# A recurrent layer with a channel-mixing layer behind it: the Vector engine's residual additions at the end of the step, their statistics in the next

## The chip, the cores and the metric

The kernel runs on one core of one Trainium2 chip. A time is the device time of one execution of the whole program in microseconds (us). Three executions of the kernel before took 246.79, 247.10 and 247.14 us; their median is 247.1.

The engines are named as the profile names them: PE is TensorE (PEld its weight loads), DVE is VectorE, ACT is ScalarE, POOL is GpSimd, SP is SyncE.

## The reference

The input x is 8 sequences of 512 tokens with 128 channels, in float32. Two layers are applied, each as "x plus the layer norm of the layer's result for the layer norm of x":

```python
x = x + _layernorm(attn(_layernorm(x)))     # gated linear recurrence, 32 heads
x = x + _layernorm(ffn(_layernorm(x)))      # token shift and channel mixing
...
# attn: proj = x @ W_in gives z, x_raw, B, C, dt, lambda, theta
x_raw = silu(x_raw); Bm = rms(Bm) * bias; Cm = rms(Cm) * bias   # B and C then turned by an angle (cumulative sum of dt * theta)
y = y_intra + y_inter                       # within a chunk, and from the state carried between chunks
y = rms(y * silu(z)); return y @ W_out
...
# ffn
xr = mu_r * x + (1 - mu_r) * x_prev; xk = mu_k * x + (1 - mu_k) * x_prev
r = sigmoid(xr @ W_r.T); k = xk @ W_k.T
out = r * (square(relu(k)) @ W_v.T)
```

The first "x plus" is the residual addition that this case is about. Its result is normalized again for the second layer, for which a mean and a variance of every token are needed.

## The kernel before, in words

**Tiles and groups.** The work is cut into 32 tiles of 128 rows: a tile holds a chunk of 64 tokens of two sequences. Four tiles (one chunk position c of all 8 sequences) are a group; there are 8 groups. Everything stays in SBUF: `x_all` holds x and later x after the first layer, `o_all` the first layer's result and later the output.

**Steps.** After a preparation of some 50 us each engine runs its own program of steps, one for a tile, n = 0 to 31, with q = n % 4. All instruction orders are written out by hand; the engines meet only through semaphores. On DVE a step does this, in this order:

- for tile n: `mask` (L1405, the scores by the causal mask, `sg`); for tile n-1: `gated_y` (L1424, `y`) and `state` (L1413, `sp`)
- `ffn(n)`: work of the second layer and of the seam between the layers, one part for each q
- for tile n+1: `weighted_x`, first half (L1398, `x`); for tile n+2: `biased` (L1381, `bc`); for tile n+1 the second half (L1398, `xg`)
- in a step with q = 3: `mix` (L1509, `curT` and `prevT`, the token shift of the group two back), which PE's product with the key weights (L1114) waits for
- for tile n+2: `rotations` (L1386 `rot`, L1391 `turned_bc`).

**The parts of `ffn` on DVE.** With c = n // 4:

- q = 0: `moments(c - 2)`: L1488 aggregates the statistics, L1490 adds epsilon; POOL then takes the power -1/2 (L500, `frs`)
- q = 1: `norm_biases(c - 2)` (L1499, `fnb`) and, from n = 17 on, `last_residual(c - 4)` (L1531, four additions into `o_all`)
- q = 2: `factor_terms(c - 1)` (L1460 to L1464, `tokc`), and from n = 14 on `gated_v` and `stats3` (L1518, L1525)
- q = 3: `residual(c - 1)` (L1471: four instructions, each x plus a factor by o, for one tile of 128x128) and `stats2(c - 1)` (L1477: four statistics of the sums). This holds for n = 7, 11, 15, 19, 23 and 27. Groups 6 and 7 are done at the end, by other calls.

**What the x product hangs on.** `weighted_x` for tile n+1 reads the bank into which PE projects tile n+1 (L876, three products) and on which ACT applies silu (L667). PE may start that projection only when DVE has released the bank with the second half (`xg`) for tile n. So there is a ring DVE, PE, ACT, DVE, gone round once in a step. PE does other work in between: the turn of B and C (L940), the projection of B, C and z (L868), the turn of y (L1062, after DVE's `y`), the mixing (L975, L963, L969), the scores (L954) and the output (L1071).

**POOL** has in each step the lower part of the projected tile (L430), a power (L458), the weights `wx` (L466), the product for `zs` (L473, two tensors in SBUF) and the new state `st` (L481, the same). **ACT** has in a step with q = 3 also the scaled copies for `mix` (L746, `behind`). Its squares (L656) wait for DVE's `bc` and are the first link of POOL's power and `wx` of that step.

Of the kernel before, what the change touches and what calls it, by code (L numbers as in the profile page):

```python
# [31 lines left out]
NC_ = T // L  # L32
NQ = B // 2
# [54 lines left out]
def build(nc, x, w_in, a_log, dt_bias, bc_bias, w_out, w_r, w_k, w_v, mu, consts, out, force_general=False):  # L88
    ctx = ExitStack()
    with ctx:  # L90
# [6 lines left out]
        def at(buf, i):  # L97

            if isinstance(i, int):
                return buf[:, i, :]  # L100
            return buf[:, bass.ds(i, 1), :].rearrange("p a n -> p (a n)")

        def wait_past(eng, semaphore, value):

            if not isinstance(value, int) or value > 0:
                eng.wait_ge(semaphore, value)
# [106 lines left out]
        def within(n):  # L213

            return not isinstance(n, int) or 0 <= n < NT
# [15 lines left out]
        def carries(i):  # L231

            return not isinstance(i, int) or i < NT - NQ
# [69 lines left out]
        def valid(c):  # L303

            return 0 <= c < NC_
# [5 lines left out]
        def lo(u):  # L311
            return UNITS[u][0]

        def hi(u):

            return UNITS[u][1] if u >= 0 else 0
# [21 lines left out]
        def n_of(u):  # L338
            return hi(u) - lo(u)
# [8 lines left out]
        def column2(i):  # L348

            return i // NQ % 2 * 2 * NQ + i % NQ  # L350

        def column3(i):
            return column2(i) + NQ
# [4 lines left out]
        for u2, u3 in ((7, -1), (8, -1), (-1, 5), (-1, 6), (-1, 7), (-1, 8)):  # L358
            first, n = (column2(lo(u2)), n_of(u2)) if u2 >= 0 else (column3(lo(u3)), n_of(u3))
# [8 lines left out]
        def last_use(k):  # L368

            for j in range(k - 1, -1, -1):  # L370
                if rounds[j][0] < rounds[k][1] and rounds[k][0] < rounds[j][1]:
                    return j + 1, hi(rounds[j][2]), hi(rounds[j][3])
            return 0, 0, 0

        def aggregated(k):

            return sum(r[1] - r[0] for r in rounds[:k + 1])
# [849 lines left out]
        def _(dve):  # L1227
# [155 lines left out]
            def rotations(n, q):  # L1383
                dve.wait_ge(S["bc_ready"], n + 1)

                vec.tensor_tensor(rot[:], bc[:].rearrange("p (g a n) -> p g a n", g=G3, a=2).unsqueeze(3)  # L1386
                                  .broadcast_to([128, G3, 2, 2, H]),
                                  at(cs_all, n).rearrange("p (a j n) -> p a j n", a=2, j=2).unsqueeze(1)
                                  .broadcast_to([128, G3, 2, 2, H]), ALU.mult).then_inc(S["rotated"], 1)
                dve.wait_ge(S["rotated"], n + 1)  # L1390
                vec.tensor_tensor(turned_bc[:, q].rearrange("p g (j n) -> p g j n", j=2), rot[:, :, 0], rot[:, :, 1],  # L1391
                                  ALU.add).then_inc(S["bc_turned"], 1)
# [63 lines left out]
            def factor_terms(u):  # L1456
                t = tiles_in(u)
                dve.wait_ge(S["o_sb"], hi(u))
                dve.wait_ge(S["ysq_done"], hi(u))
                vec.scalar_tensor_tensor(out=tokc[:, 1, t], in0=ysq_all[:, t, 0], scalar=EPS_LN, in1=osq_all[:, t, 0],  # L1460
                                         op0=ALU.mult, op1=ALU.add).then_inc(fac_v, 1)
                vec.tensor_tensor(tokc[:, 2, t], csq_all[:, t, 0], eps_all[:, t], ALU.add).then_inc(fac_v, 1)
                dve.wait_ge(fac_v, FAC_STEPS * u + 2)
                vec.scalar_tensor_tensor(out=tokc[:, 6, t], in0=tokc[:, 2, t], scalar=EPS_LN * EPS_RMS * SCALE2_INV,  # L1464
                                         in1=tokc[:, 1, t], op0=ALU.mult, op1=ALU.add).then_inc(fac_v, 1)

            def residual(u):

                dve.wait_ge(fac_p, u + 1)
                for i in range(lo(u), hi(u)):  # L1470
                    vec.scalar_tensor_tensor(out=x_all[:, i], in0=o_all[:, i], scalar=tokc[:, 7, i:i + 1],  # L1471
                                             in1=x_all[:, i], op0=ALU.mult, op1=ALU.add).then_inc(C["x1"], 1)

            def stats2(u):
                for i in range(lo(u), hi(u)):
                    dve.wait_ge(C["x1"], i + 1)
                    vec.bn_stats(fst[:, column2(i)], x_all[:, i]).then_inc(C["stats"], 1)  # L1477

            def moments(k):

                used, n2, n3 = last_use(k)
                wait_past(dve, C["norm_bias"], used)
                wait_past(dve, C["pow"], used)
                wait_past(dve, C["stats"], hi(rounds[k][2]))
                wait_past(dve, C["stats3"], hi(rounds[k][3]))
                t = slice(rounds[k][0], rounds[k][1])
                for j in range(t.start, t.stop):
                    vec.bn_aggr(fag[:, j], fst[:, j]).then_inc(C["agg"], 1)  # L1488
                dve.wait_ge(C["agg"], aggregated(k))
                vec.tensor_scalar(fmo[:, t], fag[:, t, 1], EPS_LN, None, ALU.add).then_inc(C["mom"], 1)  # L1490

            def norm_biases(k):

                used, n2, n3 = last_use(k)
                dve.wait_ge(C["pow"], k + 1)
                wait_past(dve, C["normed"], n2)
                wait_past(dve, C["outv"], n3)
                t = slice(rounds[k][0], rounds[k][1])
                vec.scalar_tensor_tensor(out=fnb[:, t], in0=fag[:, t, 0], scalar=-1.0, in1=frs[:, t], op0=ALU.mult,  # L1499
                                         op1=ALU.mult).then_inc(C["norm_bias"], 1)  # L1500
# [12 lines left out]
            def gated_v(u):  # L1513
                dve.wait_ge(C["th"], u + 1)
                dve.wait_ge(C["v_ps"], u + 1)
                wait_past(dve, C["res"], hi(ahead(u)))
                for k, i in enumerate(range(lo(u), hi(u))):
                    vec.scalar_tensor_tensor(out=ff[:, slot(i)], in0=th[:, slot(i)], scalar=1.0,  # L1518
                                             in1=ffn_bank("v", u)[:, k * D:k * D + D],
                                             op0=ALU.add, op1=ALU.mult).then_inc(C["f"], 1)  # L1520
# [6 lines left out]
            def last_residual(u):  # L1527
                dve.wait_ge(C["pow"], round3(u) + 1)
                dve.wait_ge(C["x1"], hi(u))
                for i in range(lo(u), hi(u)):  # L1530
                    vec.scalar_tensor_tensor(out=o_all[:, i], in0=ff[:, slot(i)], scalar=frs[:, column3(i):column3(i) + 1],  # L1531
                                             in1=x_all[:, i], op0=ALU.mult, op1=ALU.add).then_inc(C["res"], 1)

            def ffn(n):
                c, q = divmod(n, NQ)
                if q == 0 and valid(c - 2):
                    moments(c - 2)
                if q == 1 and valid(c - 2):
                    norm_biases(c - 2)
                if q == 1 and valid(c - 4):  # L1540
                    last_residual(c - 4)
                if q == 2 and valid(c - 1):
                    factor_terms(c - 1)
                if q == 2 and valid(c - 3):
                    gated_v(c - 3)
                    stats3(c - 3)
                if q == 3 and 0 <= c - 1 < NC_ - 2:
                    residual(c - 1)
                    stats2(c - 1)

            def last_ffn(general):
                stats2(6)
# [37 lines left out]
            def step(n, q, general):  # L1590
                if within(n) and not general:
                    mask(n)
                if within(n - 1):
                    if general:
                        tokens_general(n - 1, (q - 1) % NQ, (q + 1) % 2)
                    gated_y(n - 1, (q - 1) % NQ, (q + 1) % 2, general)
                    if not general and carries(n - 1):
                        state(n - 1, (q - 1) % NQ)
                if within(n) and general:
                    mask(n)  # L1600
                ffn(n)
                if within(n + 1):
                    weighted_x(n + 1, (q + 1) % 2, 0)
                if within(n + 2) and not (isinstance(n, int) and n == -2):
                    biased(n + 2)
                if within(n + 1):
                    weighted_x(n + 1, (q + 1) % 2, 1)
                if q == NQ - 1 and valid(n // NQ - 2):
                    mix(n // NQ - 2)
                if within(n + 2):  # L1610
                    rotations(n + 2, (q + 2) % NQ)

            biased(0)

# [57 lines left out]
```

## Time and profile before

| | |
|---|---|
| median of three runs | 247.1 us |
| the profiled execution: its own time | 247.12 us |
| its span, from the first to the last instruction | 245.3 us |
| around the span | 247.12 - 245.3 = 1.82 us |
| mean granted clock of TensorE | 0.960 |
| DVE busy / PE busy | 210.7 us (86%) / 208.8 us (85%) |
| ACT busy / POOL busy | 181.3 us (74%) / 142.4 us (58%) |

The page divides the span into 40 slices of 6.1 us. From the slice at 116 us to the one that ends at 202 us DVE's digits are all nines, which means 90% busy or more; PE's are nines and a few sevens. The chain that ended last holds only three pieces at the end of the program, so it says nothing of the middle; the steps have to be read from the timelines. In a timeline a row is a run of equal instructions of one engine. The duration of an instruction runs until its result is out; the next one on DVE usually starts 0.07 to 0.1 us before that. A bracket gives the idle time of the engine ahead of the row and what ended it.

### The profile page before, as it was taken

How to read it: one execution, taken by the hardware profiler on the slowest of the kernel's cores; microseconds unless marked ns; L12 is line 12 of the kernel's file. 1: busy time of each engine (PE TensorE's matmuls, PEld its weight loads, DVE VectorE, ACT ScalarE, POOL GpSimd, SP SyncE). 2: the span in 40 equal slices, each digit the busy share in tenths (PEclk: the TensorE clock that was granted, in tenths of full speed). 3: DMA queues.
4: the chain of work that ended last, by engine and by line, in shares of the span. 5: the costliest groups of instructions: out<-in, count | busy, mean ns of one | idle time of the engine just before them, and what ended most of it. 6: DMA issues, size and time to landing. Idle time of an engine off the chain costs nothing. (4 is left out here: it accounts for less than half of the span.)

```text
span 245.3 us, 6409 instructions
## 1 busy us (share of the span) xinstructions
PE 208.8 (85%) x1902; PEld 156.1 (64%) x1902; DVE 210.7 (86%) x658; ACT 181.3 (74%) x697; POOL 142.4 (58%) x241
## 2 busy tenths in 40 slices
PE   0895997589999999979979997999799799949930
PEld 0893443357777776758857875787588577627920
DVE  1799999987879987996999999999999998864880
ACT  2466685639988689778977896899789879747661
POOL 7444225646777696766757765766777576046230
PEclk9999799989999999999999999999999999986995
DMA  5980000000000000000000001001000100100223
GB/s 119 233 283 1 3 0 0 1 0 4 3 1 4 0 3 0 4 1 3 3 3 0 3 4 44 3 0 45 3 3 0 43 5 4 43 0 0 45 52 88
DMA packets 10199, 6.45 MB, mean 26 GB/s; under 512 B 864, under 2 KB 9856, under 8 KB 10160
## 3 DMA queue, kind: packets, MB, share of 16 engines
q1 hardware_dynamic: 10016, 5.77, 9.1%
q8 instruction: 18, 0.29, 0.5%
q0 software_dynamic: 144, 0.21, 0.4%
q14 instruction: 21, 0.17, 0.2%
HBM read 3.88 MB, written 2.10 MB: 24 GB/s over the span
## 5 line engine op out<-in xcount | busy, mean ns | idle before, releaser
L975 PE MATMUL bank<-x,sg 64*64 64x256 f32 x256 | 35.4, 396 | 0.0
L667 ACT ACTIVATE bank<-bank,rsn 128x512 f32<-128x512 f32 x32 | 21.1, 659 | 17.0 <-PE bank L876 17.0
L975 PE MATMUL bank<-xg,sg 64*64 64x256 f32 x256 | 33.0, 376 | 0.0
L963 PE MATMUL pair<-x,turned_bc 64*64 64x256 f32 x224 | 31.1, 397 | 0.0
L1398 DVE TENSOR_TENSOR x<-bank,wx 128x512 f32<-128x512 f32 x32 | 21.8, 682 | 7.3 <-ACT bank L667 7.3
L458 POOL TENSOR_TENSOR rb<-mse,halfn 128x2 f32<-128x2 f32 x32 | 24.8, 773 | 2.5
L500 POOL TENSOR_TENSOR frs<-fmo,halfn 128x8 f32<-128x8 f32 (+2 forms) x13 | 15.1, 1158 | 17.2 <-DVE fmo L1490 17.2
L1071 PE MATMUL bank<-wo_sb,yt 128*128 128x128 f32 x128 | 23.3, 306 | 1.9 <-ACT yt L683 1.9
L430 POOL TENSOR_TENSOR x_lo<-xnT_all,x_hi 128x128 fp32r<-128x128 f32 x32 | 14.8, 463 | 17.0 <-ACT x_hi L582 16.9
L656 ACT ACTIVATE junk<-bank 128x64 f32<-128x64 f32 x64 | 13.9, 228 | 11.2 <-DVE bc L1381 8.7
L975 PEld LDWEIGHTS bank<-xg,sg 64*64 64x64 f32 x256 | 18.0, 134 | 6.3 <-issue 0.2
L473 POOL TENSOR_TENSOR zs<-zs,ec_all 128x256 f32<-128x256 f32 x32 | 22.0, 687 | 0.0
L975 PEld LDWEIGHTS bank<-x,sg 64*64 64x64 f32 x256 | 15.4, 135 | 10.1 <-issue 6.1
L1398 DVE TENSOR_TENSOR xg<-bank,wx 128x512 f32<-128x512 f32 x32 | 21.7, 679 | 0.0
L455 POOL TENSOR_TENSOR mse<-msb,eps_all 128x2 f32<-128x2 f32 x32 | 7.4, 233 | 24.0 <-ACT junk L658 23.8
L481 POOL TENSOR_TENSOR st<-sp,f_all 128x256 f32<-128x256 f32 x28 | 18.1, 646 | 5.4 <-DVE sp L1413 5.4
L876 PE MATMUL bank<-w_hi,x_hi 128*128 128x512 f32 x32 | 17.2, 536 | 3.8 <-DVE w_lo L1282 2.7
L1071 PEld LDWEIGHTS bank<-wo_sb,yt 128*128 128x128 f32 x128 | 17.1, 194 | 4.7 <-ACT yt L683 2.1
L969 PE MATMUL bank<-st,bt 64*64 64x256 f32 x128 | 19.4, 379 | 0.6 <-DVE o_all L1333 0.6
L954 PEld LDWEIGHTS pair<-bt 64*64 64x64 f32 x256 | 16.9, 132 | 4.4
L954 PE MATMUL pair<-bt 64*64 64x64 f32 x256 | 18.0, 217 | 0.0
L1386 DVE TENSOR_TENSOR rot<-bc,cs_all 128x384 f32<-128x384 f32 x32 | 17.6, 550 | 0.0
(200 smaller groups left out, 712.0 us busy)
## 6 DMA issues: line engine op xcount, KB each, us to landing
x_all<-x SPq DMA_DIRECT2D x16, 128.0 KB, 3.7
out<-o_all SPq DMA_DIRECT2D x14, 128.0 KB, 2.5
cm<-consts SPq DMA_DIRECT2D x1, 640.0 KB, 5.6
w_sb<-w_in SPq DMA_DIRECT2D x1, 480.0 KB, 4.6
out<-o_all SPq DMA_DIRECT2D x4, 64.0 KB, 2.1
cm<-consts POOLq DMA_DIRECT2D x1, 128.0 KB, 3.9
wo_sb<-w_out SPq DMA_DIRECT2D x1, 128.0 KB, 4.7
bcb_sb<-bc_bias SPq DMA_DIRECT2D x1, 96.0 KB, 3.7
```

The source lines that it names most:

```text
L458: nc.gpsimd.tensor_tensor(rb[:, par], mse[:], halfn[:, 0:R], ALU.pow).then_inc(S["rb_ready"], 1)
L473: nc.gpsimd.tensor_tensor(zs[:, q].rearrange("p (h e) -> p h e", e=P), zs[:, q].rearrange("p (h e) -> p h e", e=P), at(ec_all, n).unsqueez ...
L481: nc.gpsimd.tensor_tensor(st[:, q].rearrange("p (h e) -> p h e", e=P), sp[:].rearrange("p (h e) -> p h e", e=P), at(f_all, i).unsqueeze(2) ...
L667: nc.scalar.activation(x_ps[:], x_ps[:], ACT.Silu, scale=rsn[:, par:par + 1]).then_inc(S["x_silu"], 1)
L876: mm = nc.tensor.matmul(x_ps[:], a[:, par], b[:, O_X:O_S], start=(k == 0), stop=(k == 2))
L954: mm = nc.tensor.matmul(scores[half(h), r], bt[half(r), par, r, half(h)], bt[half(r), par, 1 - r, half(h)], start=True, stop=True)
L963: mm = nc.tensor.matmul(p_ps[half(1 - h)], turned_bc[half(h), q, 2 * r], rx(x, r)[half(h)], start=(r == 0), stop=(r == R - 1))
L969: mm = nc.tensor.matmul(y_ps[par][half(h)], bt[half(1 - h), par, h, half(h)], state[half(1 - h)], start=True, stop=stop)
L975: mm = nc.tensor.matmul(y_ps[par][half(h)], sg[half(h), a, r], rx(x, r)[half(h)], start=start, stop=stop)
L1071: mm = nc.tensor.matmul(o_ps, yt[:, k], wo_sb[:, k], start=(k == 0), stop=(k == 1))
L1386: vec.tensor_tensor(rot[:], bc[:].rearrange("p (g a n) -> p g a n", g=G3, a=2).unsqueeze(3) .broadcast_to([128, G3, 2, 2, H]), at(cs_all, ...
L1398: vec.tensor_tensor((x1, xg)[a][:, par].rearrange("p (a e) -> p a e", e=P), x_ps[:].rearrange("p (a e) -> p a e", e=P), wx[:, par, a].unsq ...
```

## The change

In the steps with q = 3 the four residual additions leave the front (behind `sp`) and go to the end (behind `turned_bc`). Their four statistics go to the next step, q = 0, directly ahead of the aggregation. Only DVE's order is changed; the orders of PE, ACT, POOL and SP stay, and no instruction is added or removed.

```diff
             def ffn(n):
                 c, q = divmod(n, NQ)
                 if q == 0 and valid(c - 2):
+                    if c - 2 < NC_ - 2:
+                        stats2(c - 2)
                     moments(c - 2)
...
-                if q == 3 and 0 <= c - 1 < NC_ - 2:
-                    residual(c - 1)
-                    stats2(c - 1)
...
             def step(n, q, general):
...
                 if within(n + 2):
                     rotations(n + 2, (q + 2) % NQ)
+                if q == NQ - 1 and 0 <= n // NQ - 1 < NC_ - 2:
+                    residual(n // NQ - 1)
```

The front of a step with q = 3 on DVE, as the order of instructions has it (`sp` is the new state's sum, `x` the first half of the x product, `bc` the biased B and C):

```order
 L1424 TENSOR_TENSOR y<-bank,zs 128x256
 L1413 TENSOR_TENSOR sp<-pair,st 128x256
-L1471 SCALAR_TENSOR_TENSOR x_all<-o_all,tokc,x_all 128x128 x4
-L1477 BN_STATS fst<-x_all 128x6 x4
 L1398 TENSOR_TENSOR x<-bank,wx 128x512
 L1381 TENSOR_TENSOR bc<-bank,bcb_sb 128x192
```

The additions and statistics are gone from between `sp` and the x product.

The end of the same step and the front of the next on DVE (`turned_bc` is the last instruction of the step before; `sg` and `y` open the next step, `fag` is the aggregation):

```order
 L1386 TENSOR_TENSOR rot<-bc,cs_all 128x384
 L1391 TENSOR_TENSOR turned_bc<-rot 128x192
-L1405 TENSOR_TENSOR sg<-pair,cm 128x256
-L1424 TENSOR_TENSOR y<-bank,zs 128x256
-L1413 TENSOR_TENSOR sp<-pair,st 128x256
+L1471 SCALAR_TENSOR_TENSOR x_all<-o_all,tokc,x_all 128x128 x4
+L1405 TENSOR_TENSOR sg<-pair,cm 128x256
+L1424 TENSOR_TENSOR y<-bank,zs 128x256
+L1413 TENSOR_TENSOR sp<-pair,st 128x256
+L1477 BN_STATS fst<-x_all 128x6 x4
```

The additions now stand between `turned_bc` and `sg`, and the statistics between `sp` and the aggregation.

## Rows read from the trace of the kernel before

**Rows 1.** The page's part 1: busy us, share of the span, instructions, by engine.
```profile
PE 208.8 (85%) x1902; PEld 156.1 (64%) x1902; DVE 210.7 (86%) x658; ACT 181.3 (74%) x697; POOL 142.4 (58%) x241
```

**Rows 2.** Windows: busy us (instructions) by engine, clock, DMA share, GB/s; one group.
```profile
122.00:144.30 22.30, 20.89 (x225) 16.41 (x225) 22.09 (x69) 18.05 (x78) 15.57 (x28) 1.00 0.01 2
```

**Rows 3.** Timeline of DVE, step 15: start us, us, engine, line, work, [idle].
```profile
122.60 0.42 DVE L1413 TENSOR_TENSOR sp<-pair,st 128x256 f32<-128x256 f32 x1
122.93 1.89 DVE L1471 SCALAR_TENSOR_TENSOR x_all<-o_all,tokc,x_all 128x128 f32<-128x128 f32 x4
124.75 0.86 DVE L1477 BATCH_NORM_STATS2 fst<-x_all 128x6 f32<-128x128 f32 x4
125.53 0.67 DVE L1398 TENSOR_TENSOR x<-bank,wx 128x512 f32<-128x512 f32 x1
...
126.98 0.74 DVE L1509 SCALAR_TENSOR_TENSOR curT<-bank,mu_sb,behind 128x512 f32<-128x512 f32 x1
127.64 0.74 DVE L1509 SCALAR_TENSOR_TENSOR prevT<-bank,mu_sb,behind 128x512 f32<-128x512 f32 x1
...
128.87 0.44 DVE L1391 TENSOR_TENSOR turned_bc<-rot 128x192 f32<-128x192 f32 x1
...
129.57 0.41 DVE L1424 TENSOR_TENSOR y<-bank,zs 128x256 f32<-128x256 f32 x1
```

**Rows 4.** Timeline of ACT, the same step.
```profile
123.45 0.66 ACT L667 ACTIVATE bank<-bank,rsn 128x512 f32<-128x512 f32 x1 [0.66 <-PE bank L876]
...
124.50 1.27 ACT L746 ACTIVATE behind<-bank,one_less_mu 128x512 f32<-128x512 f32 x2
125.64 0.40 ACT L683 ACTIVATE yt<-bank 128x256 f32<-128x256 f32 x1
126.49 0.22 ACT L656 ACTIVATE junk<-bank 128x64 f32<-128x64 f32 x1 [0.45 <-DVE bc L1381]
```

**Rows 5.** Timeline of PE's matmuls and weight loads, steps 15 and 16.
```profile
128.43 1.12 PE L1114 MATMUL bank<-curT,wk_sb 128*128 128x512 f32 x2 [1.41 <-DVE prevT L1509]
...
130.71 0.34 PEld L1062 LDWEIGHTS bank<-cm,y 128*128 128x128 f32 x2
```

**Rows 6.** Timeline of DVE: x's first product in steps 9, 10, 13, 17, 29; curT.
```profile
92.12 0.69 DVE L1398 TENSOR_TENSOR x<-bank,wx 128x512 f32<-128x512 f32 x1 [0.82 <-ACT bank L667]
...
97.36 0.69 DVE L1398 TENSOR_TENSOR x<-bank,wx 128x512 f32<-128x512 f32 x1 [1.17 <-ACT bank L667]
...
114.06 0.69 DVE L1398 TENSOR_TENSOR x<-bank,wx 128x512 f32<-128x512 f32 x1 [1.79 <-ACT bank L667]
...
136.40 0.68 DVE L1398 TENSOR_TENSOR x<-bank,wx 128x512 f32<-128x512 f32 x1
...
203.31 0.69 DVE L1398 TENSOR_TENSOR x<-bank,wx 128x512 f32<-128x512 f32 x1 [0.92 <-ACT bank L667]
...
213.06 0.75 DVE L1509 SCALAR_TENSOR_TENSOR curT<-bank,mu_sb,behind 128x512 f32<-128x512 f32 x1 [1.22 <-ACT behind L746]
```

**Rows 7.** Timeline of POOL, steps 15 and 16.
```profile
123.01 0.76 POOL L473 TENSOR_TENSOR zs<-zs,ec_all 128x256 f32<-128x256 f32 x1
123.73 0.68 POOL L481 TENSOR_TENSOR st<-sp,f_all 128x256 f32<-128x256 f32 x1
...
128.35 0.75 POOL L466 TENSOR_TENSOR wx<-w_all,rb 128x128 f32<-128x128 f32 x1
129.06 0.74 POOL L473 TENSOR_TENSOR zs<-zs,ec_all 128x256 f32<-128x256 f32 x1
```

**Rows 8.** Line L1471 in step 15, then behind step 30: durations ns min/median/max.
```profile
L1471 DVE SCALAR_TENSOR_TENSOR x_all<-o_all,tokc,x_all x4: 339/533/726, 122.9 to 124.5; 128x128 f32<-128x128 f32 x4
...
L1471 DVE SCALAR_TENSOR_TENSOR x_all<-o_all,tokc,x_all x4: 338/342/343, 210.0 to 210.8; 128x128 f32<-128x128 f32 x4
```

**Rows 9.** Timeline of DVE at the end: the statistics directly ahead of their aggregation.
```profile
214.39 0.86 DVE L1477 BATCH_NORM_STATS2 fst<-x_all 128x6 f32<-128x128 f32 x4
215.45 0.64 DVE L1488 BATCH_NORM_AGGREGATE fag<-fst 128x2 f32<-128x6 f32 x8 [0.20 <-DVE fst L1477]
```

## The prediction

> **What bounds the kernel now.** First the page's busy shares [rows 1]: DVE 86% and PE 85%, so neither idles much, and the shares alone do not tell which of them an idle piece would hurt. The chain that ended last is of no use here. So I went to the windows: a group of four steps with all of the second layer's work takes 22.3 us, and in it DVE is busy for 22.09 and PE for 20.89 [rows 2]; the two groups behind it look alike. From step 15 to step 28 DVE has no gap at all in its timeline. PE has about 1.4 us to spare in a group, and it spends them in one place: ahead of the key's product, which waits for DVE's `prevT` (1.41 us idle) [rows 5]. ACT and POOL are well below. So from step 15 to step 28 each 0.1 us that DVE idles or works longer counts, unless a later idle place swallows it. Such places are the x products of steps 9, 10 and 13 (0.82, 1.17 and 1.79 us idle, waiting for ACT's silu), of step 29 (0.92), and `curT` behind step 31's work (1.22) [rows 6]. In step 17 the x product at 136.40 waits for nothing, because `last_residual` fills that place from there on.
>
> **The change part by part.** I number by step 15, whose rows are shown.
>
> 1. The x product comes too early. The additions and statistics stood in front of it, from 122.93 to 125.53, 2.60 us [rows 3]. They covered the wait for silu, which ended at 123.45 + 0.66 = 124.11 [rows 4]; DVE follows 0.03 later (in step 13 the like is seen), at 124.14. Now DVE gets there at 122.93 and idles 124.14 - 122.93 = 1.21 us.
>
> 2. Then `curT`. It stands 126.98 - 125.53 = 1.45 behind x, which would be 125.59. It needs ACT's `behind`, done at 124.50 + 1.27 = 125.77 [rows 4], say 125.80. Another 0.21. Together DVE is 1.42 us late.
>
> 3. The aggregation now stands right behind the statistics that it waits for. Elsewhere a successor on DVE starts some 0.08 us before the end of the instruction ahead; at the end of the kernel, where this very pair stands together, the statistics end at 214.39 + 0.86 = 215.25 and the aggregation starts at 215.45 after 0.20 idle [rows 9]. So the pair costs 0.20 to 0.28 us; I take 0.25, once a group. From above the bound is that 0.28, from below nothing. For steps 16, 20 and 24: 3 x 0.25 = 0.75.
>
> The Trainium skill says otherwise: in "VectorE: DVE Perf Modes", section "The DRAIN you can't avoid", a semaphore after each operation is told to cost nothing over having it only after the last, since the pipe is emptied anyway. By that the 0.75 would be 0 and the sum 247.25, the first rival. The trace has the 0.20 us gap on exactly this pair, so the row decides.
>
> 4. Whom the additions meet. Four additions take 338 to 343 ns each where POOL is idle, behind step 30, and 339 to 726 in step 15 [rows 8]. Started 0.26 apart they would need 1.05 us; in step 15 they hold the engine for 124.75 - 122.93 = 1.82, so 0.77 are lost. The two long ones end just behind POOL's `zs` (123.01 + 0.76) and `st` (123.73 + 0.68) [rows 7]. I read it so: an addition with two SBUF tensors and a POOL instruction on SBUF tensors take turns. At the new place `wx` and `zs` are due. POOL's `wx` starts 128.35 - 125.53 = 2.82 behind x, `zs` 3.53 behind it to 4.27 [rows 3, 7], and both hang on DVE's `bc` through ACT's squares, so they move along with x. The additions will start 128.87 - 125.53 + 0.28 = 3.62 behind x: into the end of `wx` and the whole of `zs`. In step 15 itself the squares cannot start before ACT's `yt` is over at 126.04 [rows 4], so POOL is later by some 0.8 and both meetings are whole. Bounds for a group: -0.77 (no meeting) to +0.4 (held up by `wx` in full and `zs` in full, and `turned_bc` too). I take +0.1 for each of steps 15, 19 and 23: 0.3. The same instructions in `last_residual` meet POOL before and after; I take no change.
>
> 5. What is gained. The statistics no longer stand ahead of the next step's `sg` and `y`: 125.53 - 124.75 = 0.78, and `turned_bc` no longer collides with `wx` (128.87 to the next at 129.23, 0.36 where 0.28 is usual): 0.86 in all. PE's turn of y starts at 130.71, though `y` was there at 129.57 + 0.41 = 129.98 [rows 3, 5]: PE was 0.73 late because it had waited for `prevT`. With the additions and statistics no longer ahead of it, `prevT` comes 2.60 earlier, less the lateness of DVE, so PE has its key's product behind it in time and takes y as it comes. So this point of PE stands at DVE's lateness - 0.86 - 0.73.
>
> **Paid once, not in each group.** Once DVE is 1.42 late to PE, the x product of step 19 finds silu done: PE stands at 1.42 - 0.86 - 0.73 = -0.17, so silu's end is not later than before, 1.21 behind DVE's old arrival, and DVE arrives 1.42 or more later than that. The cover that the additions gave is now given by DVE's own lag. The same holds for steps 23 and 27. The lag of steps 7 and 11 never gets that far: 1.42 + 0.25 = 1.67 is less than 0.82 + 1.17 and less than 1.79, the idle times behind them [rows 6]. I count 0.0 for both.
>
> **The sum.** At step 28's turn of y on PE: 1.42 + 0.75 + 0.30 - 0.86 - 0.73 = +0.88 us. From there to the end PE leads. DVE is late by 1.42 + 0.25 x 4 + 0.1 x 4 = 2.8; step 29's x product absorbs 0.92 of that, so 1.9 is left, and the wait of 1.22 ahead of `curT`, whose end moves with PE by 0.88 (together 2.1), takes it. The end then hangs on ACT's `behind` as before. So +0.9 on the profiled execution's 247.12 (span 245.3 and 1.82 around it), which is the median of 247.1 within 0.02: **248.0 us**.
>
> **The rivals.**
>
> - *Nothing that can be measured.* The aggregation waits for nothing more (0 for 0.75), or the additions meet POOL a little less: 247.12 + 0.88 - 0.75 = 247.25. For it: only 0.13 us separates it from a change too small to see, and gains and losses here are of one size. Against it: the gap of 0.20 at the very same pair [rows 9].
> - *Faster.* The additions slip past POOL. One mechanism: `wx` and `zs` are over before `turned_bc`, or both start only behind the additions. Then a group gains 0.77; with four of them up to step 28, 0.88 - 0.30 - 4 x 0.77 = -2.5, that is 244.6. It shows in the median of L1471 near 345 ns instead of 530. It decides from two groups on. For it: the new place has no `st`, which waits for `sp` of the next step. Against it: `zs` at 3.53 to 4.27 behind x, the additions at 3.62.
> - *Much slower: the stall is paid in each group.* If PE is held back by DVE's lateness as much as DVE is late (for instance because the projection waits for `xg` in steps 16 to 18 and silu moves too), 1.21 + 0.21 come again in steps 19, 23 and 27: 3 x 1.42 = 4.3 on top, 252.3. For it: DVE has no spare time in the group. Against it: PE's 1.4 us of spare time [rows 5], which is more than the 0.88.
>
> **How the numbers follow.** A difference of 0.2%, 0.5 us, is about what a measurement of this kernel tells from no change. Forecast (247.5 to 249.0 as its own range) 0.47, of it nearly all slower by more than that: 0.45, and 0.02 within. No change 0.26. Faster 0.18. Much slower 0.09. So faster 0.18, within 0.2% 0.28, slower 0.54. The range leaves out half of the faster case's sum, down to 246.2, since one or two groups may slip past POOL rather than all, and goes up to 249.5, where the +0.4 bound for three groups (+0.9 more) and some of a second stall fit.
>
> **What the changed profile would show.** Right, if the x product of step 15 idles about 1.2 us for silu and that of step 19, 23 and 27 (nearly) nothing; `curT` in step 15 0.2 for `behind`; the aggregations about 0.2 idle behind the statistics; L1471's median still above 450 ns; the idle time ahead of the key's product below its 1.41 in step 15; steps 9, 10 and 13 with less idle time than now; the idle of step 29's x product gone. Wrong, if step 19 stalls again by more than 0.5 (then the third rival), if L1471 falls to some 345 ns (the second), or if the aggregation starts without a gap (the first). It would also be wrong if the steps up to 14 lose time, which I count at zero.

## The result, and the profile after

The changed kernel takes 252.5 us (median of 4 runs, 251.8 to 253.2), the kernel before 247.1 beside it: a ratio of 1.0223 [1.0188 to 1.0257]. That is slower by 5.5 us, where 248.0 was forecast with a range up to 249.5. The profiled execution took 253.19, with a span of 251.4 against 245.3: 6.1 us more in the trace.

The page's part 1 after, answering to [rows 1]:

```profile
PE 210.7 (84%) x1902; PEld 155.6 (62%) x1902; DVE 210.3 (84%) x658; ACT 181.5 (72%) x697; POOL 141.5 (56%) x241
```

DVE is busy for 210.3 us (210.7 before). The span grew by 6.1 us with no instruction added, and the busy shares of both DVE and PE fell: on DVE this is waiting, not work. Two rows of the list of waits say where (us in total, times, longest), first of before, then of after:

```profile
DVE x L1398 <- ACT bank L667: 7.3, 8, 1.8
...
PE pair L940 <- DVE sg L1405: 3.1, 4, 1.5
```

```profile
DVE x L1398 <- ACT bank L667: 12.0, 13, 1.5
...
PE pair L940 <- DVE sg L1405: 9.4, 10, 1.8
```

The x product's wait for silu grew by 4.7 us, in 5 more places.

**Where it was lost.** I set the two traces level at the x product of step 3, where the changed kernel stood 0.4 later with nothing of the change in front of it, and compared the starts of the x products behind it. In steps 9 and 13, where DVE waits in both kernels, after is 0.16 and 0.12 ahead. Then it is behind by 1.2 in step 16, 3.1 in step 20, 4.9 in step 24 and 6.7 in step 28. So the group of step 15 costs some 1.3 us, and the three groups behind it 1.85, 1.87 and 1.77. The four x products with q = 3 from step 15 on, on DVE's timeline of after (start us, us, idle before in brackets):

```profile
124.40 0.69 DVE L1398 TENSOR_TENSOR x<-bank,wx 128x512 f32<-128x512 f32 x1 [1.13 <-ACT bank L667]
...
148.59 0.69 DVE L1398 TENSOR_TENSOR x<-bank,wx 128x512 f32<-128x512 f32 x1 [1.46 <-ACT bank L667]
...
172.79 0.69 DVE L1398 TENSOR_TENSOR x<-bank,wx 128x512 f32<-128x512 f32 x1 [1.47 <-ACT bank L667]
...
196.89 0.69 DVE L1398 TENSOR_TENSOR x<-bank,wx 128x512 f32<-128x512 f32 x1 [1.47 <-ACT bank L667]
```

Steps 7 and 11 wait too, 0.97 and 1.12, and lose nothing by it. Before, the four stood at 125.53, 147.85, 170.19 and 192.52 with no idle time: one group took 22.33, now 24.2 (the last 24.1). The prediction had the first of the four waits (1.21 forecast, 1.13 measured) and none of the others. The group from step 19 on, as the windows have it, before (answering to [rows 2], which is the group ahead of it) and after:

```profile
147.85:170.19 22.34, 21.06 (x228) 16.28 (x224) 22.13 (x69) 19.08 (x83) 15.60 (x27) 1.00 0.06 14
```

```profile
148.59:172.79 24.20, 21.64 (x226) 16.02 (x230) 22.23 (x68) 19.14 (x82) 15.41 (x27) 1.00 0.05 13
```

DVE's busy time rose by 0.10, its idle time from 0.21 to 1.97: 1.76. Of the new idle time 1.47 is the wait for silu, 0.20 the aggregation's, and 0.1 stands ahead of `curT`.

The rest of it on DVE's timeline of after, steps 19 and 20:

```profile
149.46 0.68 DVE L1398 TENSOR_TENSOR xg<-bank,wx 128x512 f32<-128x512 f32 x1
150.24 0.75 DVE L1509 SCALAR_TENSOR_TENSOR curT<-bank,mu_sb,behind 128x512 f32<-128x512 f32 x1
...
152.15 0.36 DVE L1391 TENSOR_TENSOR turned_bc<-rot 128x192 f32<-128x192 f32 x1
152.43 1.65 DVE L1471 SCALAR_TENSOR_TENSOR x_all<-o_all,tokc,x_all 128x128 f32<-128x128 f32 x4
154.00 0.41 DVE L1405 TENSOR_TENSOR sg<-pair,cm 128x256 f32<-128x256 f32 x1
...
154.66 0.41 DVE L1413 TENSOR_TENSOR sp<-pair,st 128x256 f32<-128x256 f32 x1
155.00 0.86 DVE L1477 BATCH_NORM_STATS2 fst<-x_all 128x6 f32<-128x128 f32 x4
156.05 0.64 DVE L1488 BATCH_NORM_AGGREGATE fag<-fst 128x2 f32<-128x6 f32 x8 [0.20 <-DVE fst L1477]
```

`curT` starts 0.78 behind the start of `xg`; in the same step of before it was 0.59 (148.71 to 149.30), so 0.19 is lost to the wait for `behind`. The additions take 1.65 here, less than the 1.89 of before. The aggregation idles 0.20 behind the statistics, as [rows 9] had it. PE's key product, answering to the first row of [rows 5]:

```profile
127.52 1.13 PE L1114 MATMUL bank<-curT,wk_sb 128*128 128x512 f32 x2 [0.23 <-DVE prevT L1509]
```

Its idle time fell from 1.41 to 0.23 in step 15 (0.46 in step 19, where DVE is later).

**What silu of step 19 waits for.** ACT's timeline of before, step 18 to the silu of step 19 at 146.12:

```profile
142.93 0.22 ACT L656 ACTIVATE junk<-bank 128x64 f32<-128x64 f32 x1 [0.52 <-DVE bc L1381]
...
143.78 0.48 ACT L673 ACTIVATE zs<-bank,rsn 128x256 f32<-128x256 f32 x1
...
144.55 1.27 ACT L774 ACTIVATE o_all<-o_all,fnb 128x128 f32<-128x128 f32 x4
...
146.12 0.66 ACT L667 ACTIVATE bank<-bank,rsn 128x512 f32<-128x512 f32 x1
```

And of after:

```profile
144.71 0.22 ACT L656 ACTIVATE junk<-bank 128x64 f32<-128x64 f32 x1 [0.56 <-DVE bc L1381]
...
145.55 0.47 ACT L673 ACTIVATE zs<-bank,rsn 128x256 f32<-128x256 f32 x1
...
146.32 1.27 ACT L774 ACTIVATE o_all<-o_all,fnb 128x128 f32<-128x128 f32 x4
...
147.90 0.66 ACT L667 ACTIVATE bank<-bank,rsn 128x512 f32<-128x512 f32 x1
```

"Silu of step 19" is the one whose result the x product of step 19 reads. In both kernels the squares wait for `bc`, DVE's own instruction in step 18, and silu starts 3.19 us behind the first square (146.12 - 142.93, 147.90 - 144.71; for step 23 of after it is 3.21). No idle time stands between: ACT works through `zs`, the squares of y, then `outputs` (L774, 1.27 us) and the late output, and silu is next in its queue. PE's projection for it was over by then: its last product ended at 145.19 + 0.39 = 145.58 before and at 146.76 + 0.39 = 147.15 after, 0.54 and 0.75 ahead of silu. Compare silu of step 15, in after:

```profile
122.51 0.28 ACT L693 ACTIVATE o_all<-bank 128x128 f32<-128x128 f32 x1
...
123.71 0.66 ACT L667 ACTIVATE bank<-bank,rsn 128x512 f32<-128x512 f32 x1 [0.66 <-PE bank L876]
```

There it waited for PE's projection, and `outputs` is absent (it runs from step 18 on). I had read step 15 and written the rule down for all.

### The profile page after: what moved, and what is told of

Read it like the earlier page. It is cut to its first block and busy times, and to the rows that moved or that the text cites. A ratio compares the mean times of both kernels' runs of the same rounds, so it can differ in the third digit from the quotient of the medians.

```text
span 251.4 us, 6409 instructions
## 1 busy us (share of the span) xinstructions
PE 210.7 (84%) x1902; PEld 155.6 (62%) x1902; DVE 210.3 (84%) x658; ACT 181.5 (72%) x697; POOL 141.5 (56%) x241
## 5 line engine op out<-in xcount | busy, mean ns | idle before, releaser
L975 PE MATMUL bank<-x,sg 64*64 64x256 f32 x256 | 34.6, 389 | 0.0
L963 PE MATMUL pair<-x,turned_bc 64*64 64x256 f32 x224 | 30.3, 389 | 0.0
L458 POOL TENSOR_TENSOR rb<-mse,halfn 128x2 f32<-128x2 f32 x32 | 25.4, 794 | 2.5
L455 POOL TENSOR_TENSOR mse<-msb,eps_all 128x2 f32<-128x2 f32 x32 | 8.1, 254 | 24.6 <-ACT junk L658 24.2
L473 POOL TENSOR_TENSOR zs<-zs,ec_all 128x256 f32<-128x256 f32 x32 | 20.8, 649 | 0.0
L940 PE MATMUL pair<-cm,turned_bc 128*128 128x128 f32 x64 | 12.6, 278 | 9.4 <-DVE sg L1405 9.4
L940 PEld LDWEIGHTS pair<-cm,turned_bc 128*128 128x128 f32 x64 | 7.8, 140 | 17.6 <-issue 14.2
```

The costliest lines, as they stand in the source:

```text
L458: nc.gpsimd.tensor_tensor(rb[:, par], mse[:], halfn[:, 0:R], ALU.pow).then_inc(S["rb_ready"], 1)
L473: nc.gpsimd.tensor_tensor(zs[:, q].rearrange("p (h e) -> p h e", e=P), zs[:, q].rearrange("p (h e) -> p h e", e=P), at(ec_all, n).unsqueez ...
L940: mm = nc.tensor.transpose(t_ps[:, 128 * k:128 * k + 128], turned_bc[:, q, k:k + 2].rearrange("p g n -> p (g n)"), c_("ident"))
L963: mm = nc.tensor.matmul(p_ps[half(1 - h)], turned_bc[half(h), q, 2 * r], rx(x, r)[half(h)], start=(r == 0), stop=(r == R - 1))
L975: mm = nc.tensor.matmul(y_ps[par][half(h)], sg[half(h), a, r], rx(x, r)[half(h)], start=start, stop=stop)
```

## The experiments

Experiments 1 to 7 and 9 tell readings of the loss apart; the others look for the version that should be kept. Theory A, in the expectations, is the first reading that I took from the two traces. A ratio is to the kernel before, run on the same chip in the same session (its median there 246.2 to 246.7).

**1. Only the statistics move.** The additions stay at the front of the step with q = 3.

```diff
 (against the kernel before)
                 if q == 0 and valid(c - 2):
+                    if c - 2 < NC_ - 2:
+                        stats2(c - 2)
                     moments(c - 2)
...
                     residual(c - 1)
-                    stats2(c - 1)
```

> Half of the change: the four additions stay at the front of the step with q = 3, only their statistics go to the next step. In the changed kernel a group of four steps takes 24.2 us instead of 22.33. Theory A (a ring: x product of q = 3, the rest of DVE's work up to `bc` of q = 1, ACT's squares, `normed`, late_o, PE's turn of y in q = 2, projection, silu, x product) has the additions' 1.6 us out of the ring again: 24.2 - 1.6 = 22.6, the statistics' wait costs 0.25 a group: 248.1 us (247.6 to 248.6). Theory B (PE's turn of B and C, L940, waits for `sg`, which the additions delay) expects `sg` earlier than before: 247.2 to 248.1. If the statistics and their wait were the cause, it would stay near 252.

Measured: 246.0 us, ratio 0.9966 [0.9942, 0.999]. A miss on the good side (247.6 to 248.6 was expected). No x product with q = 3 waits: the additions alone are cover enough. The pair's gap is there:

```profile
151.29 0.86 DVE L1477 BATCH_NORM_STATS2 fst<-x_all 128x6 f32<-128x128 f32 x4
152.35 0.64 DVE L1488 BATCH_NORM_AGGREGATE fag<-fst 128x2 f32<-128x6 f32 x8 [0.20 <-DVE fst L1477]
```

A group takes 22.6, 0.25 more than before, as the gap says. The gain was made ahead of step 16, where this kernel is 0.9 ahead of before, and the groups behind eat it up (0.2 ahead in step 28). At the end 1.1 is there again, from steps 29 and 30: before waits 0.92 in step 29, this kernel does not.

**2. Both move into the next step.** Additions and statistics stand behind `sp` in the step with q = 0, so nothing is ahead of `sg`.

```diff
 (against the changed kernel)
                     if c - 2 < NC_ - 2:
+                        residual(c - 2)
                         stats2(c - 2)
...
-                if q == NQ - 1 and 0 <= n // NQ - 1 < NC_ - 2:
-                    residual(n // NQ - 1)
```

> Additions and statistics both in the step with q = 0, behind `sp`: `sg` and `y` no longer wait for the additions. Theory A: the additions are still between the x product of q = 3 and `bc` of q = 1, so the ring keeps its length: 24.0 to 24.2 us a group, 252 us (251.3 to 253). Theory B: PE's idle time of 1.03 us ahead of L940 in q = 0 goes and with it the loss: 247.5 to 249. Both agree that the idle time ahead of L940 goes; only the time tells.

Measured: 251.7, ratio 1.0231 [1.0191, 1.027], as slow as the changed kernel. The x product of step 19 still waits, on DVE:

```profile
148.25 0.69 DVE L1398 TENSOR_TENSOR x<-bank,wx 128x512 f32<-128x512 f32 x1 [1.48 <-ACT bank L667]
```

and on PE the turn of B and C, which the rival blamed, has no idle time ahead of it:

```profile
153.04 0.38 PE L940 MATMUL pair<-cm,turned_bc 128*128 128x128 f32 x2
```

So it is not where the additions went that costs, but that they left. That PE waits for `sg` behind the additions in the changed kernel (9.4 us in all against 3.1) is true and costs nothing here.

**3. ACT's `normed` later.** It leaves the end of the step with q = 1 for the place behind `late_yt` in the next.

```diff
 (against the changed kernel)
+                if q == 2 and valid(n // NQ - 2):
+                    normed(n // NQ - 2)
...
-                if q == 1 and valid(c - 2):
-                    normed(c - 2)
```

> The changed DVE order, and on ACT the four `normed` (L731, 1.64 us) moved from the end of the step with q = 1 to behind `late_yt` in q = 2, so that late_o and silu don't stand behind them. Theory A: the ring is cut; PE's turn of y in q = 2 (L1062) no longer idles 0.89 us for late_o, a group takes 24.2 - 0.9 = 23.3 (then the ring through `sg` and PE is next), end 253.2 - 3 x 0.9 = 250.3 (249.5 to 251). Theory B: no change, 252 to 253. If both rings are wrong and only DVE's stall counts: no change.

Measured: 252.5, ratio 1.0246 [1.0202, 1.029]. Nothing gained, so theory A fell in its first form, in which `normed` delayed PE and PE delayed silu. ACT's timeline of this kernel, step 22 (its lines stand 2 lower):

```profile
169.72 1.26 ACT L776 ACTIVATE o_all<-o_all,fnb 128x128 f32<-128x128 f32 x4
...
171.29 0.66 ACT L667 ACTIVATE bank<-bank,rsn 128x512 f32<-128x512 f32 x1
```

PE's projection was over by 169.75 (its last product starts at 169.35 and takes 0.40), 1.5 us ahead of silu. ACT's own queue held silu: `outputs`. This form of the theory (C) is the one that stayed.

**4. `last_residual` later.** The last additions go from the front of the step with q = 1 to its end.

```diff
 (against the changed kernel)
-                if q == 1 and valid(c - 4):
-                    last_residual(c - 4)
...
+                if q == 1 and valid(n // NQ - 4):
+                    last_residual(n // NQ - 4)
```

> The changed DVE order, and `last_residual` (L1531, 2.15 to 2.25 us) moved from ahead of the x product in q = 1 to the end of that step, that is behind `bc`. Theory A: 2.2 us less between the x product of q = 3 and `bc` of q = 1, so ACT's squares and all behind them come earlier; the ring through ACT falls to 22.0, the one through PE (23.3) is left: 250.3 us (249.5 to 251). Theory B: `sg` of q = 0 is as late as before, 252 to 253.

Measured: 251.7, ratio 1.022 [1.0185, 1.0254]: no change, where theory A expected 250.3 and theory B 252 to 253. The four additions became faster (1.28 for 2.2 us), but where they had stood the x product now waits, and step 23 waits as before:

```profile
160.91 0.69 DVE L1398 TENSOR_TENSOR x<-bank,wx 128x512 f32<-128x512 f32 x1 [0.75 <-ACT bank L667]
...
172.58 0.69 DVE L1398 TENSOR_TENSOR x<-bank,wx 128x512 f32<-128x512 f32 x1 [1.46 <-ACT bank L667]
```

A second cover taken away with the like result: 0.75 of new waiting ate what the additions gave.

**5. ACT's `outputs` later.** From the step with q = 2 to the one with q = 3.

```diff
 (against the changed kernel)
-                if q == 2 and valid(c - 4):
+                if q == 3 and valid(c - 4):
                     outputs(c - 4)
```

> Theory C, formed after the first four: the x product of steps 19, 23 and 27 waits for ACT, and ACT's silu stands at a fixed distance behind DVE's own `bc` of the step before: squares, zs, ysq, then the four `outputs` (L774, 1.26 us) and late_o; 3.19 us from the first square to silu, in the kernel before (142.93 to 146.12) as in the changed one (144.71 to 147.90). DVE has only 2.8 us of its own between, so the 1.46 us are paid in every group, however late DVE is. Here: the changed DVE order, and `outputs` moved from the end of the step with q = 2 to the end of q = 3, off that path. Theory C: the stall of steps 19, 23 and 27 falls from 1.46 to 0.2 to 0.6, a group from 24.19 to 22.7 to 23.3, the time to 248.0 to 249.7. Theories A and B (rings through several steps, through `normed` or through `sg`): unchanged at 251.5 to 253.

Measured: 250.6, ratio 1.0151 [1.0116, 1.0186]; a group takes 23.53. The right direction, short of what was expected (248.0 to 249.7): the wait fell from 1.46 to 0.83, not to 0.2 to 0.6. Timeline of this kernel, silu and x product of step 23, and PE's turn of y one step earlier:

```profile
166.89 0.41 PE L1062 MATMUL bank<-cm,y 128*128 128x128 f32 x2 [0.89 <-ACT junk_o L695]
...
171.16 0.66 ACT L667 ACTIVATE bank<-bank,rsn 128x512 f32<-128x512 f32 x1 [0.40 <-PE bank L876]
...
171.86 0.69 DVE L1398 TENSOR_TENSOR x<-bank,wx 128x512 f32<-128x512 f32 x1 [0.83 <-ACT bank L667]
```

With `outputs` gone silu waits for the projection, which is late because the turn of y waited for ACT's `late_o`, which stands behind `normed` (1.64 us), which stands behind the squares of step 21, which wait for `bc` of step 21. So there are two chains from an earlier `bc` to silu; the first (through `outputs`) ends 0.63 later than the second. Experiment 3 had cut the second while the first still held.

**6. Control: the same edit on the kernel before.**

```diff
 (against the kernel before)
-                if q == 2 and valid(c - 4):
+                if q == 3 and valid(c - 4):
                     outputs(c - 4)
```

> The control: the kernel before with the same move of `outputs` alone. Theory C: silu is over before DVE comes to the x product there (the additions and statistics cover it), DVE is without a gap, so nothing changes: 247.0 within 0.4. If moving `outputs` is worth something by itself, the gain shows here too, and the fall in the other run is no proof.

Measured: 246.7, ratio 0.9999 [0.998, 1.0018]. The move is worth nothing by itself; what it gave in 5 was part of the loss.

**7. The change for the first two groups only.** Steps 7 and 11 as in the changed kernel, the others as before.

```diff
 (against the changed kernel)
-                    if c - 2 < NC_ - 2:
+                    if c - 2 < 2:
                         stats2(c - 2)
...
+                if q == 3 and 2 <= c - 1 < NC_ - 2:
+                    residual(c - 1)
+                    stats2(c - 1)
...
-                if q == NQ - 1 and 0 <= n // NQ - 1 < NC_ - 2:
+                if q == NQ - 1 and 0 <= n // NQ - 1 < 2:
```

> The change only for groups 0 and 1 (steps 7 and 11); from step 15 on the order of the kernel before. All theories: steps 7 and 11 stall by 0.97 and 1.12 us, but steps 9, 10 and 13 idle less in return; x of step 13 comes 0.25 later than before. So 247.3 (247.0 to 247.6) for a kernel before at 247.06, the loss is made from step 15 on.

Measured: 246.5, ratio 0.9997 [0.9976, 1.0017]. The x product of step 11 waits 1.13 us, and from step 15 on the kernel is 0.1 to 0.2 ahead of before. The whole loss is in the four groups from step 15 on; where DVE waits anyway a step later, a wait earlier is free.

**8. Keep the cover, break the pair.** The additions stay at the front, the statistics go between `y` and `sp` of the next step, so that `sp` stands between them and the aggregation.

```diff
 (against the kernel before)
                     residual(c - 1)
-                    stats2(c - 1)
...
                     gated_y(n - 1, (q - 1) % NQ, (q + 1) % 2, general)
+                    if q == 0 and 0 <= n // NQ - 2 < NC_ - 2:
+                        stats2(n // NQ - 2)
                     if not general and carries(n - 1):
                         state(n - 1, (q - 1) % NQ)
```

> The half that made the kernel faster (statistics in q = 0, additions at the front of q = 3), with the statistics one place earlier, between `y` and `sp`, so that `sp` stands between them and the aggregation. The gap of 0.20 us behind the statistics should go: a group 22.58 - 0.28 = 22.3, and the 1.5 us won up to step 15 are kept: 0.8 to 1.1 us below the run with the statistics behind `sp`, ratio 0.992 to 0.996 to the kernel before. Against it: `sp` is 0.78 later, and with it POOL's state; if that counts, no gain over the other.

Measured: 243.7, ratio 0.9885 [0.9856, 0.9915]: better than both kernels, and than expected (0.992 to 0.996). DVE's timeline, step 20:

```profile
149.73 0.86 DVE L1477 BATCH_NORM_STATS2 fst<-x_all 128x6 f32<-128x128 f32 x4
150.51 0.41 DVE L1413 TENSOR_TENSOR sp<-pair,st 128x256 f32<-128x256 f32 x1
150.83 0.63 DVE L1488 BATCH_NORM_AGGREGATE fag<-fst 128x2 f32<-128x6 f32 x8
```

and its window over the group from step 19 on:

```profile
145.44:167.52 22.08, 21.26 (x230) 16.16 (x226) 21.88 (x68) 19.15 (x83) 15.30 (x27) 1.00 0.06 14
```

The aggregation starts without a gap, at 0.32 behind the start of `sp`, and a group takes 22.1, 0.5 less than in 1. Read from start to start over the instructions of a group, 0.29 of that is the pair and 0.20 the last additions (L1531), which hold DVE for 1.87 instead of 2.07 since they meet POOL differently. That second part was not expected. The kernel is 1.4 ahead of before in step 16 and 2.7 in step 30. The group is 0.26 shorter than before's, where DVE works 0.25 less.

**9. The changed kernel with both moves on ACT** (3 and 5 together).

```diff
 (against the changed kernel)
+                if q == 2 and valid(n // NQ - 2):
+                    normed(n // NQ - 2)
...
-                if q == 1 and valid(c - 2):
-                    normed(c - 2)
-                if q == 2 and valid(c - 4):
+                if q == 3 and valid(c - 4):
                     outputs(c - 4)
```

> The changed DVE order with both moves on ACT at once: `outputs` from q = 2 to the end of q = 3, and `normed` from q = 1 to behind `late_yt` in q = 2. Alone the first took the stall of steps 19, 23 and 27 from 1.46 to 0.83 us and a group from 24.19 to 23.54, the second took nothing. Theory C with its second limb (behind `outputs` stands another fixed distance: `bc` of q = 1, squares, `normed`, late_o, PE's turn of y in q = 2, PE, silu): with both limbs cut the stall falls to 0.0 to 0.3, a group to 22.6 to 22.9, the time to 247.3 to 248.7. If something else (PE's turn behind `sg` in q = 0, 1.03 us idle) also holds the x product, it stays at 23.3 or more and 250 us.

Measured: 248.8, ratio 1.0111 [1.0086, 1.0136]; a group takes 23.02. All are just outside what was expected (0.0 to 0.3 of wait, 22.6 to 22.9 a group, 247.3 to 248.7). The x product of step 23:

```profile
169.03 0.69 DVE L1398 TENSOR_TENSOR x<-bank,wx 128x512 f32<-128x512 f32 x1 [0.31 <-ACT bank L667]
```

The wait is 1.46 with both chains in place, 1.46 with `normed` moved, 0.83 with `outputs` moved, and 0.31 with both moved, and 1.2 of the 1.86 us of a group come back. What silu waits for now is in ACT's timeline of this kernel:

```profile
166.31 0.22 ACT L656 ACTIVATE junk<-bank 128x64 f32<-128x64 f32 x1 [0.44 <-DVE bc L1381]
...
168.33 0.67 ACT L667 ACTIVATE bank<-bank,rsn 128x512 f32<-128x512 f32 x1
```

ACT has no idle time between the two, and PE's projection was over at 167.95. So it is still the first chain, from DVE's `bc` of the step before through ACT's queue, with 2.02 us in place of 3.19: moving `outputs` shortened it and did not cut it.

About 0.7 us a group is left against the kernel before. Read from start to start over the instructions of one group (steps 16 to 20), it is 0.38 for this wait (0.31 idle, 0.07 of lost overlap), 0.27 for the pair, 0.18 for `curT`'s wait for `behind` and 0.22 for slower last additions (L1531), less 0.23 for the faster additions of L1471, 0.10 behind `turned_bc` and 0.08 ahead of the x product of step 20.

**10. The same two moves on the kernel of 8.**

```diff
 (against the kernel of 8)
+                if q == 2 and valid(n // NQ - 2):
+                    normed(n // NQ - 2)
...
-                if q == 1 and valid(c - 2):
-                    normed(c - 2)
-                if q == 2 and valid(c - 4):
+                if q == 3 and valid(c - 4):
                     outputs(c - 4)
```

> Additions at the front of q = 3, statistics in q = 0 between `y` and `sp` (243.67 us), with both moves on ACT. DVE is without a gap from step 14 on there, so theory C expects nothing: 243.7 within 0.5. It is the base for the two runs beside it.

Measured: 243.9, ratio 0.9893 [0.9863, 0.9923]. The time is that of 8: with the cover in place, no x product from step 15 on waits. As a control it is less clean than 6, for the equal times hide two differences. This kernel is 2.2 ahead of before in step 16, where 8 is 1.4 ahead, and then takes 22.37 a group for 22.08, since its additions (L1471) hold DVE for 2.01 instead of 1.81 and `turned_bc` costs 0.10 more.

**11. Additions directly behind `xg`**, with the moves of 10, where POOL has nothing to do.

```diff
 (against the kernel of 10)
                 if q == 3 and 0 <= c - 1 < NC_ - 2:
-                    residual(c - 1)
...
                     weighted_x(n + 1, (q + 1) % 2, 1)
+                if q == NQ - 1 and 0 <= n // NQ - 1 < NC_ - 2:
+                    residual(n // NQ - 1)
```

> The same as the run beside it, with the additions moved from the front of q = 3 to directly behind `xg`, where POOL has no instruction on SBUF tensors due. Two things are told apart. The price of meeting POOL: the four additions should hold DVE 1.05 us instead of 1.82 (median of L1471 near 345 ns). The cover: without them in front the x product of q = 3 waits for silu; with both limbs on ACT moved that wait should be at most 0.8 us. Gain up to 0.77 a group, 241 us, if the stall is 0; no gain, 243.5 to 244.5, if it is 0.8; if ACT's moves did not shorten the path (stall 1.4 or more): 246 or more.

Measured: 245.6, ratio 0.9981 [0.9961, 1.0001], slower than 10 by 1.8 us. A miss. DVE's timeline in step 15:

```profile
123.91 0.69 DVE L1398 TENSOR_TENSOR x<-bank,wx 128x512 f32<-128x512 f32 x1 [1.17 <-ACT bank L667]
...
125.38 1.13 DVE L1471 SCALAR_TENSOR_TENSOR x_all<-o_all,tokc,x_all 128x128 f32<-128x128 f32 x4
...
127.75 0.61 DVE L1386 TENSOR_TENSOR rot<-bc,cs_all 128x384 f32<-128x384 f32 x1
128.39 0.67 DVE L1391 TENSOR_TENSOR turned_bc<-rot 128x192 f32<-128x192 f32 x1
```

The additions are at their fastest, 4 in 1.13 us. But the x product waits again, 1.17 here and 0.47 in steps 19, 23 and 27 (where 9 had 0.31), and POOL's `wx` and `zs` now meet `rot` and `turned_bc` (0.61 and 0.67, where they take 0.55 and 0.36 in step 19 of the changed kernel). In the groups behind step 16 the trade is about even, 22.26 for 22.37: what was saved on the additions was paid to the wait and the neighbours. The 1.8 us are lost ahead of them. In step 16 this kernel is 0.3 behind before, where 10 is 2.2 ahead; its x products of steps 7, 11 and 15 wait 0.98, 1.45 and 1.17.

**12. Experiment 4's move on top of 11.**

```diff
 (against the kernel of 11)
-                if q == 1 and valid(c - 4):
-                    last_residual(c - 4)
...
+                if q == 1 and valid(n // NQ - 4):
+                    last_residual(n // NQ - 4)
```

> The same as the one before, and `last_residual` moved to the end of q = 1, where it took 1.28 us instead of 2.15 in an earlier run, with a stall of 0.75 ahead of the x product in its place. Expected within 0.5 us of the run with the additions behind `xg`: 0.9 won by not meeting POOL, 0.75 lost to the wait.

Measured: 247.0, ratio 1.0024 [0.9995, 1.0053], 1.4 slower than 11, where no more than 0.5 was expected either way. The x products with q = 1 now wait 1.07:

```profile
158.91 0.69 DVE L1398 TENSOR_TENSOR x<-bank,wx 128x512 f32<-128x512 f32 x1 [1.07 <-ACT bank L667]
...
161.24 1.27 DVE L1531 SCALAR_TENSOR_TENSOR o_all<-ff,frs,x_all 128x128 f32<-128x128 f32 x4
```

## Why the prediction was wrong

The direction held, the size did not. The step that failed is **"Paid once, not in each group"**: "Once DVE is 1.42 late to PE, the x product of step 19 finds silu done". By step:

- *1, x product too early.* Right for step 15: 1.13 for 1.21.
- *2, `curT`.* Right, 0.19 for 0.21, but in each of the four groups from step 15 on, not once.
- *3, the pair.* Right. 0.20 of idle time, as the row had it, and the statistics hold the engine for 0.86 where the instruction behind them used to start after 0.78: 0.28 in a group, 0.25 taken. Experiments 1 and 8 differ only in whether `sp` stands ahead of the statistics or behind them, and by 0.8%, some 2.0 us; six pairs at 0.28 are 1.7. The two do not measure the pair alone, though: 0.20 of the 0.51 by which their groups differ are the last additions'.
- *4, meeting POOL.* Forecast +0.1 for the additions, measured 0.24 less in a group (1.65 for 1.89), so wrong in sign. `last_residual` takes 0.20 more, for which nothing had been taken; together the two are near nothing. The median of L1471 in a group from step 11 to 27 is 412 to 414 ns, neither the "above 450" of the forecast nor the 345 of "faster".
- *5, the gain.* In part. PE's wait ahead of the key's product fell from 1.41 to 0.23 in step 15 as said, but PE does not take y "as it comes". Its turn of B and C now idles 1.04 for `sg`, which stands behind the additions, and the weights for the turn of y load at 131.02, when `y` had been there since 130.15 + 0.41 = 130.56. So 0.46 of the 0.73 are still lost there.
- *Paid once.* Wrong, and nearly all of the error: forecast 0.0 for steps 19, 23 and 27, measured 1.47 each, 4.4 us of the 6.1. The reasoning set silu against PE. PE stood well enough, but the silu of steps 19, 23 and 27 does not wait for PE. It stands behind `outputs` in ACT's queue, at a fixed 3.2 us behind squares that wait for DVE's own `bc` of the step before. Whatever holds up DVE holds up `bc` and with it silu, so being late gives no cover. In the trace of before DVE starts `bc` of step 18 at 142.55 and its additions at 145.26; silu ends at 146.12 + 0.66 = 146.78. Without the additions DVE waits the difference, 1.52, wherever the group stands in time (measured 1.46 to 1.47).
- *The first two groups.* Right (experiment 7).
- *The sum's tail.* The wait of 0.92 ahead of the x product of step 29 did vanish, and gave back some 0.6 of the 6.7 (step 29: 6.1).
- *The rivals.* "Much slower" had the price, 252.3 for a measured 252.5, with a chance of 0.09, and the wrong mechanism: PE's projection waiting for `xg`. That its 1.42 a group is near the measured 1.47 and 0.19 is luck. I held PE's 1.4 us of spare time against it, which only speaks to a chain through PE. "Nothing" fell with the 0.20 of the pair, "faster" with the additions that still meet POOL; both had the same step wrong as well.

The sum with the measured terms: 1.85, 1.87 and 1.77 on top of the 1.2 of step 16 make 6.7 at step 28; less 1.0 on the way from there to the end, 5.7, and the other 0.4 of the 6.1 between the spans lies ahead of step 3. The medians differ by 5.5.

Shown: that the wait recurs, that ACT's order sets its length (5 and 9, with 6 as the control), and that the additions were its cover (1, 8). Not settled: whether the last 0.31 us of it would go if the rest of ACT's work between `bc` and silu were moved too; no run tried it. The exact prices of the additions' meetings with POOL are read from the traces, and no run isolates them.

## What to carry to other kernels

Before work is taken from in front of a wait, follow what the wait hangs on, back to the engine itself. If it comes back to an instruction of the same engine at a fixed distance, the wait will be paid each time round, however late the engine is; lateness covers only waits on someone who runs ahead. And read the row in each stage where the engine works without a gap, not in the first one only: here ACT's `outputs`, which first run three steps behind the one I had read, made most of the wait.

## What the runs showed of the hardware that I had not expected

- DVE's additions on SBUF tensors and POOL's instructions on SBUF tensors seem to take turns as wholes, not to slow each other a little. This is a reading of the traces; no run tested it alone. An addition takes 339 ns at the least and up to 728 in steps 11 to 27 of before, 338 to 717 in those of after. Where they were moved to a place with none of POOL's large instructions beside them all are short (experiment 11, line L1471: min, median and longest in ns):

```profile
L1471 DVE SCALAR_TENSOR_TENSOR x_all<-o_all,tokc,x_all x32: 333/343/352, 84.0 to 222.1; 128x128 f32<-128x128 f32 x32
```

- The aggregation directly behind the statistics that it waits for costs 0.20 us of idle time and 0.08 of lost overlap. One instruction between takes both away (rows of experiments 1 and 8). It is not a price for every such pair: the addition of epsilon (L1490), which waits for the aggregation directly ahead of it, starts 0.03 behind its end in the changed kernel (131.87 + 0.64 = 132.51, then 132.54).
